# A state-space decoder block on one Trainium2 core: the first group's projections, taps and weight splits moved to other places in the engines' orders

## What is computed

```python
h    = x * rsqrt(mean(x * x) + EPS) * norm_w
gate, hBC, dt = split(h @ in_proj_w.T)              # 8192 gates, 8192 hidden + 2048 for B and C, 128 dt
hBC  = silu(causal_conv(hBC, conv_w, conv_b))       # four taps
M    = (C_i . B_j) * exp(cs_i - cs_j), j <= i       # one cs per head, 128 heads in 8 groups
y    = M @ (hidden * dt) + Dp * hidden
yg   = y * silu(gate)
out  = x + rmsnorm_by_group(yg) * gnorm_w @ out_proj_w.T
```

## Time and profile before

| | |
|---|---|
| median of 3 runs | 791.51 us (788.96 to 791.81) |
| the profiled execution's own time | 791.84 us |
| its span | 789.7 us |
| busy, share of the span | PE 98%, DVE 81%, ACT 76%, POOL 88% |
| chain that ended last, by engine | PE 90%, POOL 4%, DVE 3%, ACT 2%, issue 1% |
| mean granted clock of TensorE | 0.995 |

### The profile page before, as it was taken

One profiled execution on the slowest core, in us unless ns is written; L12 is line 12 of the kernel. 1 busy time (PEld: TensorE's weight loads), 2 busy tenths in 40 slices (PEclk: granted clock), 3 DMA queues, 4 the chain that ended last, 5 costly groups with the idle time before them and its releaser, 6 DMA issues.

```text
span 789.7 us, 13488 instructions
## 1 busy us (share of the span) xinstructions
PE 774.6 (98%) x4275; PEld 611.2 (77%) x4275; DVE 636.4 (81%) x753; ACT 596.5 (76%) x1055; POOL 696.3 (88%) x553
## 2 busy tenths in 40 slices
PE   8989899999999999999999999999999999999997
PEld 7767677877887777877787777877787778877765
DVE  6888787888879886889779886888778778798875
ACT  5799677788778877788678877787687877788552
POOL 6689999899889998899889998999899998899551
PEclk9999999999999999999999999999999999999999
DMA  8356243344254433444243324434343333431001
GB/s 327 119 159 209 91 135 101 128 135 133 67 160 133 133 111 115 133 131 127 74 160 127 116 99 131 135 113 129 109 133 116 122 123 100 136 114 66 1 2 54
DMA packets 58028, 94.94 MB, mean 120 GB/s; under 512 B 13168, under 2 KB 46064, under 8 KB 58000
## 3 DMA queue, kind: packets, MB, share of 16 engines
q1 hardware_dynamic: 57712, 94.06, 37.6%
q10 hardware_dynamic: 288, 0.52, 0.2%
HBM read 93.26 MB, written 1.31 MB: 120 GB/s over the span
## 4 chain that ended last, share of the span: by engine, by line
PE 90%; POOL 4%; DVE 3%; ACT 2%; issue 1%; DMA 0%; DVEq 0%; POOLq 0%; ACTq 0%
PE ps_z L1222 25%; PE ps_out L1357 21%; PE ps_h L1222 21%; PE ps_y L1344 11%; PE ps_t L1195 4%; POOL win_lo L305 1%; PE ps_out L1195 1%; PE ps_t L1367 1%; DVE conv L814 1%; DMA acc<-in_x 0%; POOL csx L343 0%; POOL wout_lo L310 0%; POOL win_hi L296 0%; PE ps_h L1330 0%; PE ps_t L1330 0%
## 5 line engine op out<-in xcount | busy, mean ns | idle before, releaser
L305 POOL TENSOR_TENSOR win_lo<-w_raw,win_hi 128x1024 fp32r<-128x1024 f32 x64 | 182.0, 2843 | 9.7 <-DMA csx<-cs_rows 4.7
L604 ACT ACTIVATE decay<-csx,cs_own 128x256 f32<-128x256 f32 (+1 forms) x512 | 184.4, 443 | 0.8
L814 DVE SCALAR_TENSOR_TENSOR conv<-ps_h,par,conv 128x510 f32<-128x510 f32 (+2 forms) x192 | 142.9, 744 | 20.0 <-ACT conv L533 15.4
L604 ACT ACT_TABLE_LOAD x63 | 80.8, 1283 | 90.0 <-PE ps_y L1344 82.0
L899 DVE TENSOR_TENSOR decay<-decay,cbm 128x1536 f32<-128x1536 f32 x64 | 145.5, 2273 | 0.3 <-ACT decay L604 0.3
L343 POOL TENSOR_SCALAR_AFFINE_SELECT csx<-csx 128x512 f32<-128x512 f32 x128 | 109.3, 877 | 2.5 <-DMA csx<-cs_rows 2.5
L958 DVE SCALAR_TENSOR_TENSOR v<-hidT,par,ps_y 128x512 f32<-128x512 f32 x64 | 47.8, 747 | 78.3 <-PE ps_y L1344 78.2
L1357 PE MATMUL ps_out<-wout_hi,y_hi 128*128 128x512 f32 x252 | 100.3, 398 | 0.0
L1344 PE MATMUL ps_y<-decay,hid_dt 128*64 128x256 f32 (+1 forms) x1024 | 97.3, 332 | 2.4 <-DVE decay L899 1.3
L1357 PE MATMUL ps_out<-wout_lo,y_hi 128*128 128x512 f32 x252 | 99.6, 395 | 0.0
L1357 PE MATMUL ps_out<-wout_hi,y_lo 128*128 128x512 f32 x252 | 99.3, 394 | 0.0
(11 more groups left out here) (323 smaller groups left out, 1509.6 us busy)
## 6 DMA issues: line engine op xcount, KB each, us to landing
w_raw<-in_wmain SPq DMA_DIRECT2D x64, 768.0 KB, 5.9
csx<-cs_rows SPq DMA_DIRECT2D x128, 256.0 KB, 3.5
bc_raw<-in_wbc SPq DMA_DIRECT2D x8, 517.0 KB, 5.3
ctx_raw<-in_ctx SPq DMA_DIRECT2D x1, 2048.0 KB, 14.5
par<-in_wpar SPq DMA_DIRECT2D x64, 4.0 KB, 3.6
bc_raw<-in_wffn SPq DMA_DIRECT2D x2, 512.0 KB, 4.9
out_x<-acc SPq DMA_DIRECT2D x4, 256.0 KB, 2.6
acc<-in_x ACTq DMA_DIRECT2D x2, 256.0 KB, 3.9
```

The lines of the kernel that those rows point to most:

```text
L305: eng.tensor_tensor(win_lo[:, r2, :], w_raw[:, r4, 0:W_IN], win_hi[:, r2, :].bitcast(f32), ALU.subtract).then_inc(low_win, 1)
L604: done = eng.activation(decay[:, r2, b, h, lo:lo + n], csx[:, r2, b, h, lo:lo + n], ACT.Exp, bias=cs_own[:, r2, t, h:h + 1])
L814: eng.scalar_tensor_tensor(out=out_b[:, :, back:], in0=src_b[:, :, 0:S - back], scalar=w[:, TAPS - 1 - back:TAPS - back], in1=out_b[:, :, ...
```

## The change

The edits touch only the first group.

1. PE (`first_pairs`): slots 0 to 6 are now written there. In slots 3 to 5 the hidden columns of pair k+1 follow the out of slot k, ahead of the scan. Slot 6 has none, and slot 7 begins with the hidden columns of pair 7 as before.
2. ACT: in slots 3 to 5 the tap of pair k+1, y_hi and square stand ahead of the exponentials. Slot 6 does exponentials, y_hi, square, the context's scaling, hidden, gates.
3. DVE: the constants go from slot 0 to the end of slot 3, and the convolution of pair k+1 stands at the end of slot k; slot 6 has none.
4. POOL: splits of pair k+2 in slot k (2 to 5), the out weights behind them, both ahead of the select. B's and C's split moves from slot 4 to slot 6. One wait for the first mask is new, before the lowering of pair 3.
5. SP: the loads of pairs 4 to 7 go out one slot sooner, ahead of that slot's rows.

```diff
 SP
-                if not (first and k < 4):
+                if not first:
...
+                if first and 3 <= k < PPG - 1:
+
+                    eng.dma_start(par[:, k + 1, :], wpar_d[s + 1]).then_inc(w_in[(k + 1) % 4], 16)
+                    eng.wait_ge(low_wout, s - 2)
+                    eng.dma_start(w_raw[:, (k + 1) % 4, :], wmain_d[s + 1]).then_inc(w_in[(k + 1) % 4], 16)
 POOL, slot 1
                     split_in(3, 1)
+                    eng.wait_ge(dve_m, 1)
                     lower_in(3, 1, 4)
 POOL, slot 2, behind select(1)
+                    eng.wait_ge(w_in[0], 64)
+                    eng.wait_ge(pe_gate, 3)
+                    split_in(0, 0)
+                    lower_in(0, 0, 5)
 POOL, slots 3 to 6
+                if first and k < PPG - 1:
+                    if k == PPG - 2:
+                        eng.wait_ge(bc_in, 16 * 2)
+                        eng.wait_ge(pe_bc, 2)
+                        eng.tensor_scalar(wbc_hi[:], bc_raw[:, 0:BC_W], 1.0, 0.0, ALU.mult, ALU.add).then_inc(hi_wbc, 1)
+                        lower_bc(2)
+                    else:
+                        eng.wait_ge(w_in[(k + 2) % 4], 32 * ((k + 2) // 4 + 1))
+                        eng.wait_ge(pe_gate, k + 1)
+                        split_in((k + 2) % 4, r2)
+                        lower_in((k + 2) % 4, r2, k + 3)
+                    if k > 3:
+                        eng.wait_ge(pe_out, k - 3)
+                    split_out(r4)
+                    lower_out(r4, k + 1)
+                    eng.wait_ge(act_exp, k)
+                    own_sums(k + 1, 1 - r2)
+                    eng.wait_ge(csx_in[1 - r2], 32 * ((k + 1) // 2 + 1))
+                    select(1 - r2)
+                    sum_squares(k, 0, k, True)
+                    return
 ACT
-                if first and k == 3:
-                    hidden(3, 3)
-                    gates(3, 3)
-                    finish_y(3, 0, 3, True)
-                    decays(3, 3)
+                if first and k < PPG - 2:
+                    hidden(k, k)
+                    gates(k, k)
+                    tap(k + 1, 0, k + 1)
+                    finish_y(k, 0, k, True)
+                    decays(k, k)
+                    return
+                if first and k == PPG - 2:
+                    decays(k, k)
+                    finish_y(k, 0, k, True)
+                    scale_context(0)
+                    hidden(k, k)
+                    gates(k, k)
                     return
 DVE
-                    constants()
                     return
...
-                if first and k == 3:
-                    combine(3, 3)
-                    scale_hidden(3, 3)
-                    mask(3, 0, 3)
-                    lower_y(3, 3)
+                if first and k < PPG - 1:
+                    combine(k, k)
+                    scale_hidden(k, k)
+                    mask(k, 0, k)
+                    lower_y(k, k)
+                    if k == PPG - 2:
+                        quantise_context(0)
+                        return
+                    conv_hidden(k + 1, k + 1)
+                    if k == 3:
+                        constants()
 PE
-                if first and k < 4:
+                if first and k < PPG - 1:
                     first_pairs(k)
...
-                if k < 3:
+                if k >= 3:
+                    project_out(k, 0, k)
+                if k < PPG - 2:
                     eng.wait_ge(low_win, k + 2)
                     eng.wait_ge(dve_conv, 3 * k + 3)
                     project(ps_h[:], win_hi[:, 1 - r2, 0:KT * P], win_lo[:, 1 - r2, 0:KT * P], pe_hid)
-                else:
-                    project_out(3, 0, 3)
...
+                if k == PPG - 2:
+                    project_group(k, 0, k)
...
+                if isinstance(s, int):
+                    eng.wait_ge(low_wout, s - 2)
                 eng.wait_ge(dve_ylo, s - 2)
```

More of the change, by code:

```diff
@@ L384, in slot @@
                     return
-                if k == 3 and not first:
+                if first and k < PPG - 1:
[20 more added lines that the diff above has]
+                if k == 3:
                     eng.wait_ge(pe_out, s - 3)
@@ L404, in slot @@
                     split_in(n4, (k + 1) % 2)
-                    if first:
-                        lower_in(n4, (k + 1) % 2, s + 2)
-                        eng.wait_ge(csx_in[1 - r2], 32 * (4 * g + (k + 1) // 2 + 1))
-                    else:
-                        eng.wait_ge(csx_in[1 - r2], 32 * (4 * g + (k + 1) // 2 + 1))
-                        lower_in(n4, (k + 1) % 2, s + 2)
+                    eng.wait_ge(csx_in[1 - r2], 32 * (4 * g + (k + 1) // 2 + 1))
+                    lower_in(n4, (k + 1) % 2, s + 2)
                     select(1 - r2)
@@ L1287, in slot, with project_group @@
                 if k >= PPG - 2 and not last:
-                    which = k - (PPG - 2)
-                    eng.wait_ge(low_wbc, g + 2)
-                    eng.wait_ge(act_gate, s + 1)
-                    project(ps_z[:], wbc_hi[:, which * KT * P:(which + 1) * KT * P],
-                            wbc_lo[:, which * KT * P:(which + 1) * KT * P], pe_bc)
+                    project_group(s, g, k)
+            def project_group(s, g, k):
+                which = k - (PPG - 2)
+                eng.wait_ge(low_wbc, g + 2)
+                eng.wait_ge(act_gate, s + 1)
+                project(ps_z[:], wbc_hi[:, which * KT * P:(which + 1) * KT * P],
+                        wbc_lo[:, which * KT * P:(which + 1) * KT * P], pe_bc)
             def turn(s, r2):
```

## The result

The changed kernel takes **796.0 us** (median of 6 runs, 795.12 to 796.82), the kernel before, beside it, 791.1 (788.96 to 791.81): ratio 1.0058, 95% interval 1.0040 to 1.0077. It is 0.6% slower. The forecast was 793.5, its own range 791.5 to 795.3 and the range with its rivals 789.0 to 797.5. What came lies outside the first and inside the second: it is the rival on the slower side, 796.4. Taken again later with 10 runs it gave 796.2 and a ratio of 1.0050 (1.0032 to 1.0069).

What follows compares the result with a forecast made beforehand. PE, busy throughout from 125 us, could win only 6.65 us lost before; new losses 0.3 + 0.3 + 2.7 + 3.7 + 1.6 = 8.6 turn 791.84 into 793.8, median 793.5 us; own range 791.5 to 795.3, with rivals 789.0 to 797.5.

Steps and rivals of the forecast that it cites:

- the rival on the slower side: Tap of pair 4 to mask of slot 4: DVE and POOL meet more often, clock falls twice; 796.4 us, chance 0.25.
- Where to look, and what there was to win: PE before 125 us: three waits and the low clock behind the third, 6.65 us in all to win.
- First, second and third scan: PE's waits for the mask there: 0.3 us at the first, 0.3 at the second, none at the third.
- Scan of slot 4: PE waits 2.7 us ahead of this scan for its mask; bounds 0.3 and 5.1.
- Clock: The lower level follows one of the two new long waits, at 1.6 us; bounds nothing to 3.2.
- Slot 6: PE waits 3.7 us there, ACT having two sets of exponentials behind one tap; 3.5 to 4.5.
- B and C's split: Moved to slot 6; the road through tap and convolution to slot 7's gate columns is covered by 1.7 us.

Runs made afterwards that it cites:

- experiment 1: The change with VectorE's twelve constants moved from the end of slot 3 to slot 5, between mask and y_lo: 791.2 us, ratio 1.000.
- experiment 2: The change with the constants back at the end of VectorE's slot 0: 793.8 us, ratio 1.0032.
- experiment 3: The change with two waits added on GpSimd, its splits in slots 3 and 4 held until VectorE's y_lo and mask: 797.4 us, ratio 1.0081.
- experiment 7: The change with constants ahead of y_lo in slot 3 and the tap of B ahead of the exponentials in slot 7: 790.25 us, ratio 0.9983.
- experiment 8: As experiment 7, with ScalarE's exponentials last in slot 6 too: 788.5 us, ratio 0.9962.
- experiment 4: The kernel before with only the constants moved, from slot 0 to the end of slot 3: 790.35 us, ratio 0.9982.
- experiment 5: The kernel before with only B and C's split moved, from slot 4 to slot 5: 792.2 us, ratio 1.0014.
- experiment 6: The kernel before with experiments 4 and 5 together and slot 7's tap of B ahead of the exponentials: 787.1 us; second time 787.8.
- experiment 9: Experiment 6 with slot 2's split of out weights ahead of the wait for rows: 787.65 us; then pair weights loaded one slot sooner too: 787.4.

## Why the prediction was right and where it failed

*Where to look, and what there was to win.* Right. Nothing changed from 125 us on, and all three waits of the earlier trace rows went.

*First, second and third scan.* I took 0.3, 0.3 and nothing; no wait is left at any (the first starts at 38.20, where I looked for 39.3; 0.84 of that is the start). Pessimistic by 0.6.

*Scan of slot 4.* Right in mechanism, size and clock both short: this is the step that failed. The term was 2.7 us and the wait measured 5.60. I put the road at 10.61 us undisturbed and the surplus by meetings at 0.99 + 1.02 + 0.42 = 2.43, with twice that as the bound. The road by rows is 10.61 + 2.23 (y_lo) + 2.23 (constants) + 0.94 (yg) = 16.0, a surplus of 5.40, which is outside the bound. PE's side was right (56.67 to 67.1, 10.4). For y_lo I took a mean of the earlier trace rows where this one met a whole lowering. The constants had no surplus at all: the three terms are those of y_lo, yg and mask, and the constants' 2.25 held the one meeting they had seen, 1.02 us beside a split of 1.05, where they could meet a lowering of 2.4. The mask met nothing (1.74 us). The bound should have been worked out from the longest operation GpSimd could be in the middle of at each of these places. Experiments 1 and 2 show the constants at this place as the cause: without them the wait is 0.24 to 0.43, with y_lo at 2.98 and 2.80.

*The kind of operation.* The Trainium skill, "SBUF — State Buffer", Who interferes with whom, says that a VectorE instruction with two SBUF inputs contends with a GpSimd instruction that reads SBUF, by what it calls an exclusive lock, and that issue order, not the operation's shape, decides who blocks. By that rule what an operation can lose does not depend on its own size, and this trace agrees: the last constant has two inputs and 128x1 elements, started 0.03 us behind a lowering of 2.38 and stood for 2.36, to its end. That is the point the constants' 2.25 missed.

*Clock.* Sized at 1.6 once, from a wait of 2.68. It fell behind both waits, and the first fall cost 2.8, because the low clock held over scan, turn and most of two passes. Both profiles of the change show it, so that they say nothing on whether it can stay away there. The second fall cost nothing that shows: slot 6 lost 3.9 with it and 3.73 in experiment 1 at the full clock, since ScalarE's road to the turn was the longer one either way.

*Slot 6.* The sum was right to 0.2: 12.8 us from hidden columns to turn against 12.74, and a loss of 3.6 to 3.9 in the change and in experiments 1, 2, 3 and 7. That ACT alone makes it was wrong. By experiment 8 the part at the scan is VectorE's road.

*B and C's split.* I gave the road to conv_bc a cover of 1.7 us. In the change itself it held. Once the wait of slot 4 is away it is short by 1.9 to 3.8 us. The working began at the gates of slot 6 and left out the select of slot 7, for which the exponentials wait.

*The start.* 0.84 us that no term had; they go with the lower clock at the start in the profile of the kernel before, and not with the change.

*The rival on the slower side.* Its place and mechanism are what came: meetings from the tap of pair 4 to the mask of slot 4, and the clock twice. That its number came so close is in part luck. Its sum was 11.5 us, against 12.6 lost. Its wait was 1.6 short and its first fall of the clock 1.2; against these stood 1.6 for a second fall that added nothing in slot 6, and the 0.84 of the start made up for most of what was still lacking. It deserved more than a quarter: on a road of twenty VectorE instructions beside a full GpSimd, the number of meetings was the least known term of all.

## What to carry to other kernels

When small VectorE operations are moved off one path, price each at the longest GpSimd operation it can land beside and not at its own size, and put them where VectorE is idle anyway. Between two orders of an engine's queue, ask first which item in it another engine waits for: one tap put ahead of eight exponentials was worth, by experiments 4 to 6, some 4 us, and the sooner splits of experiment 9 nothing. And before a wait is called gone, look at whom it was resting: taking away 5.6 us of PE's waiting filled GpSimd again and exposed 1.9 to 3.8 us three slots on.

## What was unexpected of the hardware

- One-input VectorE operations were held up beside GpSimd as well: the cast of 128x128 to bf16 took 0.47 us in the kernel before, and here, in experiment 6, 2.37, ending at 58.66 with GpSimd's lowering at 58.58. VectorE's row and GpSimd's:

```profile
56.29 2.37 DVE L911 CAST identb<-ident 128x128 bf16<-128x128 f32 x1
```

```profile
55.82 2.76 POOL L305 TENSOR_TENSOR win_lo<-w_raw,win_hi 128x1024 fp32r<-128x1024 f32 x1
```

- The length of a wait did not settle whether the lower clock followed: waits of 2.13 us (experiment 3), 2.23 (4) and 2.64 (6, second time) were followed by it, one of 2.88 (1) was not.
- The clock at the very start differs between profiles. Its lower level between 13 and 14 us goes with a first projection at 16.47 us (before), the full level with 15.63 (the change) and 15.55 (experiment 5). What decides it no run shows.
- GpSimd is held up as well: its select took 2.75 us beside VectorE's mask in experiment 2, and 1.22 in experiment 1.
